# A graph layer and a ternary feed-forward layer on one core: work of the first stage respread

## What is computed

```python
def gnn(x, src, dst, W_self, W_neigh, b):        # x is the layer norm of the input, 1250 x 512
    msg_sum = segment_sum(x[src], dst, 1250)     # 20,000 edges, sorted by dst
    deg = segment_sum(ones(20000), dst, 1250)
    neigh = msg_sum / maximum(deg, 1.0)[:, None]
    h = x @ W_self + neigh @ W_neigh + b
    h = where(h >= 0, h, 0.01 * h)
    return h / maximum(sqrt(sum(h * h, axis=1)), 1e-12)

def quantize(w, group=128):                      # each group of 128 inputs of a row
    scale = mean(abs(wg)) + 1e-5
    return clip(round(wg / scale), -1, 1) * scale

def ffn(x, w_gate, w_up, w_down):                # 512 -> 1408 -> 512
    gate, up = x @ quantize(w_gate).T, x @ quantize(w_up).T
    return (silu(gate) * up) @ quantize(w_down).T

x = x + gnn(layernorm(x), src, dst, ...)
x = x + ffn(layernorm(x), ...)
```

## Time and profile before

| | us |
|---|---|
| median of 3 runs | 365.71 (363.98 to 365.72) |
| profiled execution, its own time | 365.24 |
| its span, first to last instruction | 363.3 |
| outside the span (365.24 - 363.3) | 1.9 |
| mean granted clock of PE | 0.987 |
| busy: PE / DVE / ACT / POOL | 329.8 / 304.6 / 238.0 / 163.1 |

### The profile page before, as it was taken

The page is one execution under the profiler, slowest core; times in us unless marked ns, Lnnn a source line. Parts: engine busy times, 40 slices in busy tenths (PEclk is TensorE's granted clock), DMA queues, the critical chain, the costliest instruction groups (busy, mean ns, idle before and its releaser), DMA issues.

```text
span 363.3 us, 5834 instructions
## 1 busy us (share of the span) xinstructions
PE 329.8 (91%) x1623; PEld 249.6 (69%) x1623; DVE 304.6 (84%) x789; ACT 238.0 (66%) x637; POOL 163.1 (45%) x223
## 2 busy tenths in 40 slices
PE   1997879899999999999687999999999999999992
PEld 0443335554545578777476898989899898889991
DVE  3569999899889248999696998999999989999994
ACT  2155958899787136774656768668777678676670
POOL 7000000110010590110003466888788787799992
PEclk9999999999999999999988999999999999999998
DMA  7961322233232001200000000000000000000215
GB/s 226 291 159 33 86 58 78 68 88 87 59 82 79 3 3 35 74 22 2 0 1 2 0 3 0 3 0 0 2 3 2 0 0 3 0 3 0 73 44 169
DMA packets 9412, 16.69 MB, mean 46 GB/s; under 512 B 1062, under 2 KB 1886, under 8 KB 9378
## 3 DMA queue, kind: packets, MB, share of 16 engines
q1 hardware_dynamic: 9300, 16.21, 15.9%
q10 hardware_dynamic: 78, 0.08, 0.1%
HBM read 13.73 MB, written 2.56 MB: 45 GB/s over the span
## 4 chain that ended last, share of the span: by engine, by line
PE 58%; DVE 26%; ACT 10%; issue 3%; POOL 1%; DVEq 0%; ACTq 0%; POOLq 0%
PE bank L1320 39%; PE bank L1208 7%; PE bank L1250 5%; DVE tq_gu L901 4%; DVE hot_dst L1005 3%; ACT mag_early L690 3%; DVE tq_d L901 2%; DVE hot_src L996 2%; ACT a_t L742 2%; DVE bn L1061 2%; ACT hot_src L675 2%; DVE x_sb L1058 2%; DVE z L1040 1%; PE bank L1232 1%; PE bank L1156 1%
## 5 line engine op out<-in xcount | busy, mean ns | idle before, releaser
L1320 PE MATMUL bank<-x_hi,t_gu 128*128 128x378 f32 (+1 forms) x264 | 96.9, 367 | 3.6 <-DVE x_lo L1075 2.8
L1320 PE MATMUL bank<-x_lo,t_gu 128*128 128x378 f32 (+1 forms) x264 | 95.5, 362 | 0.0
L1208 PE MATMUL bank<-w_sb,xnT 128*125 128x512 f32 x160 | 86.9, 632 | 4.8 <-ACT z L725 4.1
L1114 DVE SCALAR_TENSOR_TENSOR g_acc<-bank,nscale,g_acc 128x378 f32<-128x378 f32 (+1 forms) x99 | 64.3, 650 | 12.1 <-PE bank L1320 10.8
L612 POOL TENSOR_SCALAR thr<-absum 128x4 f32<-128x4 f32 (+1 forms) x34 | 10.7, 315 | 121.5 <-ACT mag_early L690 97.2
L1114 DVE SCALAR_TENSOR_TENSOR u_acc<-bank,nscale,u_acc 128x378 f32<-128x378 f32 (+1 forms) x99 | 64.1, 647 | 0.0
L633 POOL TENSOR_TENSOR acc<-acc,d_one 128x378 f32<-128x378 f32 (+1 forms) x58 | 60.9, 1052 | 0.1
L643 POOL TENSOR_TENSOR hh<-sg,u_acc 128x378 f32<-128x378 f32 (+1 forms) x32 | 35.1, 1098 | 57.4 <-ACT sg L830 57.3
L1320 PEld LDWEIGHTS bank<-x_hi,t_gu 128*128 128x128 f32 x264 | 51.1, 193 | 8.1 <-DVE x_lo L1075 3.5
L1320 PEld LDWEIGHTS bank<-x_lo,t_gu 128*128 128x128 f32 x264 | 51.0, 193 | 3.6
L1167 PEld LDWEIGHTS bank<-hot_dst,hot_src 128*125 128x125 bf16 x157 | 20.8, 137 | 42.0 <-DVE hot_dst L1005 23.0
(11 more groups left out here) (136 smaller groups left out, 558.5 us busy)
## 6 DMA issues: line engine op xcount, KB each, us to landing
raw<-in_L_ffn_w_gate SPq DMA_DIRECT2D x11, 256.0 KB, 2.7
raw<-in_L_ffn_w_up SPq DMA_DIRECT2D x11, 256.0 KB, 2.6
out_x<-x_sb SPq DMA_DIRECT2D x10, 224.0 KB
raw<-in_L_ffn_w_down SPq DMA_DIRECT2D x8, 256.0 KB, 2.7
x_sb<-in_x SPq DMA_DIRECT2D x1, 1344.0 KB
w_sb<-in_L_gnn_W_neigh SPq DMA_DIRECT2D x1, 1024.0 KB, 6.0
w_sb<-in_L_gnn_W_self SPq DMA_DIRECT2D x1, 1024.0 KB, 7.3
raw<-in_L_ffn_w_down SPq DMA_DIRECT2D x4, 192.0 KB, 2.3
```

What stands on the lines that cost most here:

```text
L1114: nc.vector.scalar_tensor_tensor(out=to, in0=bank_of(u, what)[:, 0:w], scalar=nscale[:, j:j + 1], in1=to, op0=ALU.mult, op1=ALU.add).then_ ...
L1208: last = nc.tensor.matmul(to[0:TP, :], xnT[:, t, k * TP:(k + 1) * TP], w_sb[:, k, half * D:(half + 1) * D], start=k == 0, stop=k == KD - 1)
L1320: last = nc.tensor.matmul(to, w, parts[h], start=h == 0, stop=h == 1)
```

## The change

- **Source numbers.** ACT spreads each chunk's source numbers over 32 columns instead of 125 (`src_rep`, 8 x 32 elements for a batch), one slot earlier; DVE's comparison reads them four times over with a zero step and writes 8 x 128 elements to `hot_src`.
- **Chunks** are made two slots ahead by DVE instead of one.
- **Bias.** Two rows of bias go into a zeroed tile of 33 rows (`bias_f`), DVE makes a rounded row and its remainder (`bias_r`, in slot 6), and PE adds a product of ones with them at the end of each tile's part of W_self (ten products). POOL's ten additions and the semaphore for them are gone; DVE's sum now waits for ACT's copy of z.
- **Normalising** of tiles 2 to 9 goes from DVE to ACT (scale and bias, `shift0`).
- **Ternary blocks.** `LOADS1` goes from 25 to 18, so 72 blocks instead of 99 are made in the slots (ACT from slot 10, DVE from slot 14), and 60 instead of 33 beside the neighbour sums. These are dealt out by `PHASE`: 5 loads (20 blocks) before n = 0, and 4, 3, 2 and 2 loads (14, 12, 7 and 7 blocks) at the ends of iterations 0 to 3. ACT and DVE now handle the same loads at the end of the same iteration; before, DVE came one iteration behind.
- `x1_low` comes one iteration earlier on DVE.

```diff
+    LOADS1 = 18
+    PHASE = [5, 4, 3, 2, 2, 0, 0, 0, 0, 0]
...
+    bias_f = place("bias_f", [33, D], F32, "tq_gu", 18 * D * 2)
...
+    REP = 32
+    src_rep = place("src_rep", [P, SBS, SB, REP], BF16, "tq_d", 6656)
...
-        LOADS1 = 2 * NF + 3
...
-                return max(0, min(JOBS1, -(-JOBS1 * (s - lag + 1) // (SLOTS - 16))))
+                return max(0, min(JOBS1, -(-JOBS1 * (s - lag + 1) // (SLOTS - lag - 12))))
...
-        def down_jobs(n):
-
-            lo, hi = (LOADS1 + max(0, min(NL, 3 * i // 2)) for i in (n, n + 1))
-            return range(load_end[lo - 1], load_end[hi - 1])
-
+        def late_jobs(n):
+
+            lo = LOADS1 + sum(PHASE[:n])
+            return range(load_end[lo - 1], load_end[lo + PHASE[n] - 1])
...
-            sp.dma_start(bias_b[:, :], bias.rearrange("(a n) -> a n", a=1).to_broadcast([P, D])).then_inc(bias_in, 16)
+            sp.wait_ge(zeroed, 4)
+            for r in (0, 32):
+                sp.dma_start(bias_f[r:r + 1, :], bias.rearrange("(a n) -> a n", a=1)).then_inc(bias_in, 16)
...
-            pool.wait_ge(bias_in, 16)
-            pool.wait_ge(joined, NB - 1)
-            for t in range(NT):
-                pool.wait_ge(z_out, t + 1)
-                nc.gpsimd.tensor_tensor(z[:, t, :], z[:, t, :], bias_b[0:TP, :], ALU.add).then_inc(z_done, 1)
...
-                nc.scalar.activation(hot_src[:, b % SBS, 0:n, 0:TP],
-                                     src_lo[:, SB * b:SB * b + n, None].to_broadcast([P, n, TP]), ACT.Copy).then_inc(src_wide, 1)
+                nc.scalar.activation(src_rep[:, b % SBS, 0:n, :],
+                                     src_lo[:, SB * b:SB * b + n, None].to_broadcast([P, n, REP]), ACT.Copy).then_inc(src_wide, 1)
...
+                if i == 0 and 1 <= t and t + 1 < NT:
+                    act.wait_ge(shifted, 1 if t + 1 < LN_GROUPS[3][0] else 2)
+                    act.wait_ge(xn_T, t)
+                    nc.scalar.activation(xn[0:TP, (t + 1) % 2, :], x_sb[:, t + 1, :], ACT.Identity, bias=shift0[0:TP, t + 1:t + 2],
+                                         scale=rs[0:TP, t + 1:t + 2]).then_inc(normed, 1)
...
-                    for j in jobs_in(slot, 6):
+                    for j in jobs_in(slot, 10):
                         abs_of(j)
...
+            for j in late_jobs(0):
+                abs_of(j)
             for n in range(NT):
...
-                for j in down_jobs(n):
-                    abs_of(j)
+                if n < NT - 1:
+                    for j in late_jobs(n + 1):
+                        abs_of(j)
...
+                if slot == 6:
+                    dve.wait_ge(bias_in, 32)
+                    nc.vector.tensor_copy(bias_r[0:33, :], bias_f[:, :]).then_inc(bias_set, 1)
+                    dve.wait_ge(bias_set, 1)
+                    nc.vector.tensor_tensor(bias_r[32:33, :], bias_f[32:33, :], bias_r[32:33, :].bitcast(F32),
+                                            ALU.subtract).then_inc(bias_set, 1)
...
-                if i == 0 and 1 <= t and t + 1 < NT:
-                    normalize(t + 1)
...
-                    for c in chunks_in(slot + 1):
+                    for c in chunks_in(slot + 2):
...
-                for j in jobs_in(slot, 10):
+                for j in jobs_in(slot - 4, 10):
                     ternary_of(j)
...
                 dve.wait_ge(n_ready, t + 1)
-                dve.wait_ge(z_done, t + 1)
+                dve.wait_ge(z_out, t + 1)
...
+            for j in late_jobs(0):
+                ternary_of(j)
             for n in range(NT):
                 neighbour_sum(n)
...
-                if n >= 4:
-                    x1_low(n - 4)
-                for j in down_jobs(n - 1):
-                    ternary_of(j)
+                if n >= 3:
+                    x1_low(n - 3)
+                if n < NT - 1:
+                    for j in late_jobs(n + 1):
+                        ternary_of(j)
...
+                if half and k == KD - 1:
+                    if t == 0:
+                        pe.wait_ge(bias_set, 2)
+                    last = nc.tensor.matmul(to[0:TP, :], ones_r[0:33, 0:1].to_broadcast([33, TP]), bias_r[0:33, :],
+                                            start=False, stop=True)
...
-                pe.wait_ge(ternary, JOBS if down else JOBS1)
+                pe.wait_ge(ternary, JOBS if down else 2 * NF * KD)
```

More of the change, by code:

```diff
@@ L221, in gnn_ffn @@
         z_out = sem("z_out")
-        z_done = sem("z_done")
+        bias_set = sem("bias_set")
+        shifted = sem("shifted")
         src_wide = sem("src_wide")
@@ L699, in _ @@
                 t, i = divmod(slot, 8)
-                if slot == FIRST - 3:
+                if slot == FIRST - 4:
                     act.wait_ge(prep, 5)
@@ L896, in reciprocals, with shift0_of @@
                 dve.wait_ge(rstd, i + 1)
+            def shift0_of(i):
+                a, b = LN_GROUPS[i]
+                nc.vector.scalar_tensor_tensor(out=shift0[0:TP, a:b], in0=mv[0:TP, a:b, 0], scalar=-1.0, in1=rs[0:TP, a:b],
+                                               op0=ALU.mult, op1=ALU.mult).then_inc(shifted, 1)
             def ternary_of(j):
@@ L995, in _ @@
                             dve.wait_ge(src_wide, b + 1)
-                            nc.vector.tensor_tensor(hot_src[:, b % SBS, 0:n, 0:TP], iota[:, None, 0:TP].to_broadcast([P, n, TP]),
-                                                    hot_src[:, b % SBS, 0:n, 0:TP], ALU.is_equal)
+                            nc.vector.tensor_tensor(
+                                hot_src[:, b % SBS, 0:n, :].rearrange("p n (a r) -> p n a r", r=REP),
+                                iota[:, None, 0:P].rearrange("p n (a r) -> p n a r", r=REP).to_broadcast([P, n, P // REP, REP]),
+                                src_rep[:, b % SBS, 0:n, None, :].to_broadcast([P, n, P // REP, REP]), ALU.is_equal)
                         if c >= HOT:
@@ L1093, in _ @@
             shift1(NT - 2)
-            x1_low(6)
             def take(u, what):
@@ L1208, in _ @@
                 last = nc.tensor.matmul(to[0:TP, :], xnT[:, t, k * TP:(k + 1) * TP], w_sb[:, k, half * D:(half + 1) * D],
-                                        start=k == 0, stop=k == KD - 1)
+                                        start=k == 0, stop=not half and k == KD - 1)
+                if half and k == KD - 1:
[3 more added lines that the diff above has]
+                                            start=False, stop=True)
                 if k == KD - 1:
```

39 lines of the change are left out of this document (22 added, 17 removed).

## The result

| | before | changed |
|---|---|---|
| median of the runs made together | 365.62 | 379.37 |
| lowest to highest | 363.98 to 365.72 | 377.61 to 379.49 |
| span of the profiled execution | 363.3 | 377.3 |
| first stage, slot 8 to the first neighbour sum on PE | 98.6 | 96.8 |
| neighbour stage, to DVE's last sum | 54.9 | 70.4 |

The ratio is 1.0376 (95% interval 1.0334 to 1.0418): slower by 13.8 us, where 7.1 had been predicted. The direction was right, the time outside the range. The feed-forward stage is unchanged, so nearly all of it lies in two differences: the first stage gave 1.8 us back instead of 6.1, and the neighbour stage took 15.5 more instead of 13.6.

A forecast was written before the change was run, and what follows sets the result against it. PE bounds the neighbour stage almost wholly; the first stage holds 12.9 us of PE's stalls. Span 363.3 - 6.1 + 0.3 + 13.6 = 371.1, with 1.9 around it 373.0; forecast 372.8 us, range 366 to 378.

The forecast's parts named there:

- start, to slot 8: Kernel start: DVE's slot 6 and later chunks wait for the bias; between -0.5 and +1, taken as +0.3 us.
- nine bias products: First stage from slot 8 on: PE gains a bias product per tile at 0.25 us, 2.2 us in all.
- PE's idle time behind the statistics: First stage: statistics still block DVE some 4 us, but one more slot of chunks leaves about 1.2 of 2.8 us.
- idle behind the window check: First stage: about 0.7 of 2.9 us of stall stays, as DVE comes to the check earlier.
- z's stalls: First stage: PE's waits for late z, some 6 us, fall to about 2 us.
- other stalls: First stage: PE's remaining stalls, 0.7 us taken to stay.
- order of the neighbour stage: Neighbour stage: ACT and DVE take turns on the same loads and delay PE's transpositions; +13.6 us, bounds +11 to +15.
- slow clock on tile 6: Neighbour stage: slow stretch after PE's idle time, 1 to 2 us where PE bounds; swallowed behind tiles 4 and 5, so 0.
- feed-forward: Feed-forward stage after the neighbour stage: same instructions behind the same tail, 0.
- Rival 1: Neighbour stage: PE stays the bound as its early part takes in all blocks, 0 there; 359.4 us, faster; chance 0.12.
- Rival 3: First stage: DVE's new hot_src comparison costs 1.25 us, not 0.60; gain -2 instead of -6.1, 377 us; chance 0.11.
- PE's stalls: First stage: 12.9 of 97.9 us are PE's stalls; 4.6 would stay, so 8.3 us are gained.

The follow-up runs named there:

- the last three kernels: Changed kernel with bias on POOL, statistics spread, DVE one iteration behind ACT: 80 first-stage blocks with check spread 365.44, check in one burst 364.77; 72 blocks 363.84 us.
- the last kernel: Changed kernel, 72 first-stage blocks kept, with bias on POOL, statistics one tile a slot, late loads dealt out anew, DVE one iteration behind ACT: 363.84 us, ratio 0.9975.

## Why the prediction was wrong in size and right in direction

The sum was 371.1 us of span; it is 377.3. Step by step:

| step | predicted | measured |
|---|---|---|
| start, to slot 8 (one bias product, 0.56, is in it) | +0.3 | +0.4 |
| nine bias products | +2.2 | +5.1 |
| PE's idle time behind the statistics | 1.2 left | 2.1 to 2.4 |
| idle behind the window check | 0.7 left | 1.4 (slot 22, 2.51 instead of 1.08; PE idle for 0.7 of it) |
| z's stalls | 2 left | 0 |
| other stalls (the rest of the stage) | 0.7 left | 0.5 left |
| slow clock in the first stage | not priced | +1.7 |
| order of the neighbour stage | +13.6 | +13.9 |
| slow clock on tile 6 | 0 | +1.6 |
| feed-forward | 0 | 0 |

Two steps make the miss of 6.2 us: the bias product, 2.9 too little, and the slow clock, 3.3 where the sum had nothing. The stalls of the first stage nearly cancel among themselves. There is also a slip at the end of the sum: the profiled execution of before is 0.5 below the median, so 373.0 should have become 373.5 and not 372.8.

1. **The bias product was mis-sized.** I priced it by the step of twenty like products in a row (0.25 us); what was to be priced is one product that breaks into a row of others. The runs give 0.56, of which about 0.24 is its columns. The earlier trace rows had a warning: four transpositions between products cost 0.43; even that is less than the 0.56.

2. **The bursts.** "one more slot of chunks is ready, so about 1.2 of 2.8" failed. With a ring of seven chunks DVE waits for PE before its burst, and the burst just starts later. The run with one slot of lead has a stall only 0.3 us longer. That a longer ring would have made the lead worth more was not run.

3. **z's stalls** went entirely, more than I gave. The ternary rate was a cause, as said: at 80 blocks instead of 72 three of them return, 2.6 us. That took about 2 us off the error, by luck.

4. **The turns of ACT and DVE** were worked out nearly right. Counted from the stage's start, the first transposition was predicted at 30.7 us, the second at 39.3 and the third at 47.4; they are at 31.0, 39.6 and 47.7. The mechanism was tested by undoing the order with the same 60 blocks: 70.4 becomes 60.8, and 56.7 with fewer of them ahead of the first sum. Rival 1 (PE stays the bound) is far from true of this order, but the last three kernels show that it nearly holds for an order with the lag.

5. **The slow clock** was the other step that failed, and the larger one: 1.7 us in the first stage, where I did not ask for it, and 1.6 here. I said that idle time behind tiles 4 and 5 would swallow it. The stretch from 148.2 to 155.0 was swallowed so. A second one, from 168.7 to 172.1, came right behind PE's wait of 2.87 us before transposition 2. The stretch before it (the slow one stands in the first fence above):

```profile
165.00:168.60 3.60, 0.73 (x5) 0.33 (x4) 2.90 (x8) 2.40 (x6) 0.00 (x0) 1.00 0.00 0
```

From there on PE is the bound, so tile 6 took 6.6 us instead of 5.1. The comparison shows that it is this and not the order: with one slot of lead the same wait is followed by a tile 6 at clock 1.00 and 5.1 us, and the stage is 68.8 instead of 70.4. The Trainium skill (TensorE: Matmul & The Clock Gate, "Part 1: The HAM clock gate") says that throttled is the default state and that activity releases it; the trace agrees in so far as each slow stretch of the two stages begins in or behind idle time of PE, and the 1 to 2 us that the prediction named by that rule for a stretch where PE is the bound are the 1.6 measured. That no stretch followed the same stall in the run with one slot of lead, the rows here do not explain.

6. **Rival 3** is false: DVE's new comparison starts at 31.88 and the next operation at 32.48, 0.60 us as taken, with its repeated operand:

```profile
31.88 0.68 DVE L1020 TENSOR_TENSOR hot_src<-iota,src_rep 128x1024 bf16<-128x1024 uint16 x1
32.48 0.28 DVE L1031 TENSOR_SCALAR hot_dst<-iota_w,key 128x260 bf16<-128x260 uint16 x1
```

7. **A step that lay behind all of the first stage** was too simple, and nothing in the sum shows it: "PE's stalls" were counted as if each could be won by itself. In slots 8 to 22 PE and DVE hold each other up. Without bias products and slow stretch PE came to the check 2.3 us earlier than in the changed kernel; DVE ended it 1.6 us earlier (44.5 instead of 46.1) and PE's stall there grew by 0.7: a part of the gain stays, a part is waited out. My average over a node tile (8.3 us of DVE against 9.25 of PE) hid two bursts of 4 us that fall into the first three tiles.

What stays open: that DVE's load limits these slots was read from the traces, and no kernel with a lighter DVE in them was run; nor was the last kernel run without POOL's additions. Why a stall is followed by a slow stretch in one execution and not in another is open too.

## What to carry to other kernels

Two engines that hand work to each other in order should be an iteration apart: the same 60 blocks, dealt out for it, cost 6.1 us less when DVE's half came one iteration behind ACT's, and a step moved one iteration too early cost 3.4. Price an added operation by what happens between its unlike neighbours, not by its step in a row of its kind. Ask for each long wait of PE what a slow clock behind it would cost, in every stage. And before counting the stalls of the busiest engine as a gain, look at how much idle time the engine that it waits for has in that very stretch, and whether a third engine holds it up there.
